# First pass of an attention with one shared key head: for long rows, the maximum of two key chunks taken through a rectified difference

## The chip, the cores and the metric

The kernel runs on one core of a Trainium2 chip. The metric is the device time of one launch in microseconds (us); lower is better. The core has TensorE (matrix products into PSUM), VectorE, ScalarE, GpSimd and DMA queues, each with its own program, kept in step by semaphores.

## The reference, cut to what matters

Two transformer layers with adaptive layer norms work on x of 2048 tokens by 256, fp32. The change is in the first attention:

```python
q = (h @ Wq).reshape(1, 2048, 16, 16)        # 16 heads of 16
k = h @ Wk; v = h @ Wv                       # one key and one value head for all
scores = einsum('bihd,bjd->bhij', q, k) / 4
attn = softmax(where(j <= i, scores, -inf))  # causal
out = einsum('bhij,bjd->bihd', attn, v) @ Wo + bo
```

The router, the expert layer, a second mixing layer and a second expert layer that follow are untouched.

## The kernel before

`phase_front` holds the whole first attention. Queries are cut into 4 chunks of 512 (index c) and heads into 4 groups of 4 (index g). The 16 groups s = (c, g) are worked in the order c = 0..3, within it g = 0..3. A group has 4(c+1) *units*, one for each tile of 128 keys (index kt), so there are 16, 32, 48 and 64 units for c = 0, 1, 2, 3, 160 in all, numbered u.

A unit does the second pass. For two pairs of heads TensorE makes scores with keys on the partitions (`scores`, L391, two halves of 8 matmuls; four matmuls of 32 output rows stand beside each other in the array and count as one quad). Each half fills one of two PSUM buffers `sc[0]`, `sc[1]`, ScalarE takes the exponential of it (L548, up to 128x1024), and TensorE multiplies the probabilities of the unit before with the values (`values`, L407). The half may be written when the exponential of the half two before has ended (`e_done`, L387). In the last four units of a group (the diagonal ones) only 512, 384, 256 and 128 query columns are left, and GpSimd masks a block (L791).

The exponent needs each query row's maximum beforehand. The first pass makes it: for each head of a group, tile of 128 queries and key chunk of 512 (index ck = 0..c) TensorE makes scores with queries on the partitions (`first_pass`, L348, one quad of up to 512 columns) into a ring of 3 PSUM banks. VectorE reduces them: with a plain `reduce_max` (L604) for ck < c, and for the diagonal chunk with a fused add of the causal mask and maximum (L601). These are 640 chunks: 384 plain, 256 diagonal. The partial maxima of a row meet in `mneg` (L608), are split in two bf16 parts and travel by DMA into two extra rows of the query operand, so that the second pass subtracts them in its product.

The order of all this is written out by `front_schedule`. The first pass runs ahead of the second: 44 chunks before unit 0, the rest spread evenly over the units so that a group's last chunk comes 5 units before the group starts, at most 5 chunks a unit. From unit 140 on there is none. Within a unit TensorE does: scores of half 0, one chunk, scores of half 1, two chunks, the values of the unit before, the remaining chunks, and now and then an output transposition or projection (kinds A, B, C; L357, L365, L374) that shares the ring.

Of the kernel before, what the change touches and what calls it, by code (L numbers as in the profile page):

```python
# [10 lines left out]
BF = mybir.dt.bfloat16  # L11
# [149 lines left out]
RING = 3  # L161
QLOADS = 3


def front_schedule():

    groups = [(c, g) for c in range(NC) for g in range(NG)]
    units = [(s, kt) for s, (c, g) in enumerate(groups) for kt in range(TQ * (c + 1))]
    chunks = [(s, hs, qt, ck) for s, (c, g) in enumerate(groups) for hs in range(GH)
              for qt in range(TQ * c, TQ * (c + 1)) for ck in range(c + 1)]  # L170
    start = [min(u for u, (t, kt) in enumerate(units) if t == s) for s in range(len(groups))]
    upto = [sum(t <= s for t, hs, qt, ck in chunks) for s in range(len(groups))]
    NU = len(units)

    due = [(-1, PRE)] + [(start[s] - 1 - MARGIN, upto[s]) for s in range(len(groups)) if upto[s] > PRE]
    due.append((NU - 1, len(chunks)))
    issued = [0] * NU
    for (u0, n0), (u1, n1) in zip(due, due[1:]):
        for u in range(u0 + 1, u1 + 1):
            issued[u] = n0 + (n1 - n0) * (u - u0) // (u1 - u0)  # L180
    for u in range(NU - 2, -1, -1):
        issued[u] = max(issued[u], issued[u + 1] - 5)
    ready = [PRE] + issued
    order = (("A", 0), ("A", 1), ("B", 0), ("A", 2), ("B", 1), ("C", 0), ("A", 3), ("B", 2), ("C", 1), ("B", 3),
             ("C", 2), ("C", 3))
    extras = {u: [] for u in range(NU + 1)}
    for c, (first, step) in enumerate(((start[4] + 2, 1), (start[8] + 2, 1), (start[15] - 4, 1))):
        for n, (kind, t) in enumerate(order):
            extras[first + step * n].append((kind, TQ * c + t))
    extras[NU] = [(kind, TQ * (NC - 1) + t) for kind, t in order]  # L190

    entries = []
    pre, n = [], 0
    for c in range(NC):
        for count in EARLY.get(c, ()):
            pre += [("P", n + j) for j in range(count)]
            n += count
        pre.append(("V", c))
    for m in range(PRE - n):
        pre.append(("P", n + m))  # L200
        if m % 2 == 0 and m // 2 < 6:
            pre.append(("M", m // 2))
    assert ("M", 5) in pre
    for e in pre:
        entries.append(e)
    per_unit = []
    for u in range(NU + 1):
        mine = [("P", n) for n in range(ready[u], ready[u + 1])] if u < NU else []
        first = len(entries)
        entries += mine + extras[u]  # L210
        per_unit.append((list(range(first, first + len(mine))), list(range(first + len(mine), len(entries)))))
    return groups, units, chunks, start, upto, entries, len(pre), per_unit


def phase_front(nc, k, a, sem, sb):
    groups, units, chunks, start, upto, entries, NPRE, per_unit = front_schedule()
    at = {e: r for r, e in enumerate(entries)}
    NU, NS = len(units), len(groups)
    diags = {u: n for n, u in enumerate(u for u, (s, kt) in enumerate(units) if kt >= TQ * groups[s][0])}
# [3 lines left out]
    with ctx:  # L223
# [14 lines left out]
        hT = k.h[:, 2 * TQ:4 * TQ, :].rearrange("p i d -> p (i d)").rearrange("p (s t n) -> p s t n", s=2, t=KH)  # L238
        parts = sb("q_parts", [P, 2, 3, KH, QC], BF)
        ks, vaug = sb("ks", [P, T], BF), sb("vaug", [P, NT, 32])  # L240
# [19 lines left out]
        pool_step = sem("f_pool_step")  # L260
        wqd_ready = sem("f_wqd_ready")
        silu_done, col_done, col_ready, wk_ready = sem("f_silu_done"), sem("f_col_done"), sem("f_col_ready"), sem("f_wk_ready")
        var1_ready, rstd1_ready, xh_ready = sem("f_var1_ready"), sem("f_rstd1_ready"), sem("f_xh_ready")
# [21 lines left out]
        def _(pe):  # L285
# [39 lines left out]
            def mod_rows(r, n):  # L325
# [7 lines left out]
                last.then_inc(ring_done, 1)  # L333

            def first_pass(r, n):
                s, hs, qt, ck = chunks[n]
                c, g = groups[s]
                diag = ck == c
                w = (qt % TQ + 1) * P if diag else QC
                free(r)  # L340
                if n == 0 or chunks[n - 1][0] != s:
                    pe.wait_ge(part_done, 9 * (c + 1))
                    pe.wait_ge(q_in[c], 16 * QLOADS)
                    if c == 0 and g:
                        pe.wait_ge(q_rest, 16 * QLOADS)
                for j in range(4):
                    q0 = P * (qt % TQ) + 32 * j
                    last = nc.tensor.matmul(bank(r)[32 * j:32 * (j + 1), 0:w], qs[0:KROWS, c, GH * g + hs, q0:q0 + 32],  # L348
                                            ks[0:KROWS, QC * ck:QC * ck + w], start=True, stop=True,
                                            tile_position=(0, 32 * j))  # L350
                last.then_inc(ring_done, 1)

# [29 lines left out]
            def scores(u, pair):  # L382
                s, kt = units[u]
                c, g = groups[s]
                off = max(0, kt - TQ * c) * P
                if u:
                    pe.wait_ge(e_done, 2 * u + pair - 1)  # L387
                for i in range(2):
                    for j in range(4):
                        k0 = P * kt + 32 * j  # L390
                        last = nc.tensor.matmul(sc[pair][32 * j:32 * (j + 1), i, off:QC], ks[0:KALL, k0:k0 + 32],  # L391
                                                qs[0:KALL, c, GH * g + 2 * pair + i, off:QC],
                                                start=True, stop=True, tile_position=(0, 32 * j))
                last.then_inc(s_done, 1)

            def values(u):
# [3 lines left out]
                if u in diags:  # L400
                    pe.wait_ge(masked, 2 * diags[u] + 2)
                else:
                    pe.wait_ge(e_done, 2 * u + 2)
                if kt == 0 and s:
# [46 lines left out]
            for u, (s, kt) in enumerate(units):  # L451
                mine, more = per_unit[u]
                if kt == 0:
                    pe.wait_ge(rows_in[s], 16 * NROWDMA)
                scores(u, 0)
                for r in mine[0:1]:
                    entry(r)
                scores(u, 1)
                for r in mine[1:3]:
                    entry(r)  # L460
# [9 lines left out]
        def _(act):  # L470
# [38 lines left out]
            def entry(r):  # L509
# [3 lines left out]
                if kind == "B":  # L513
                    copy_norm(r, n)

            def copy_out(s):
                c, g = groups[s]
# [23 lines left out]
            for u, (s, kt) in enumerate(units):  # L541
# [4 lines left out]
                for pair in range(2):  # L546
                    act.wait_ge(s_done, 2 * u + pair + 1)
                    nc.scalar.activation(prob[:, u % 2, 2 * pair:2 * pair + 2, off:QC], sc[pair][:, :, off:QC],  # L548
                                         ACT.Exp, scale=HD ** -0.5).then_inc(e_done, 1)
                if u - 1 in last_unit:  # L550
                    copy_out(last_unit[u - 1])
# [7 lines left out]
        def _(dve):  # L559
# [34 lines left out]
            def maxima(r, n):  # L594
                s, hs, qt, ck = chunks[n]
                c, g = groups[s]
# [3 lines left out]
                if ck == c:  # L600
                    nc.vector.tensor_tensor_reduce(unread[:, r % RING, 0:w], bank(r)[:, 0:w], causal[:, QC - w:QC], 1.0, NEG,  # L601
                                                   ALU.add, ALU.max, mpart[:, s % 2, hs, t, ck:ck + 1]).then_inc(ring_used[r % RING], 1)
                else:
                    nc.vector.reduce_max(mpart[:, s % 2, hs, t, ck:ck + 1], bank(r)[:, 0:w], AX.X).then_inc(ring_used[r % RING], 1)  # L604
                if n + 1 == upto[s]:
                    for m in range(max(0, r - RING + 1), r + 1):
                        dve.wait_ge(ring_used[m % RING], uses(m))
                    step(nc.vector.tensor_reduce(mneg[:, :, :], mpart[:, s % 2, :, :, 0:c + 1], axis=AX.X, op=ALU.max,  # L608
                                                 negate=True))
# [120 lines left out]
        def _(pool):  # L730
# [12 lines left out]
            for c in range(1, NC):  # L743
# [6 lines left out]
            nc.gpsimd.affine_select(out=causal[:, QC - P:QC], in_=causal[:, QC - P:QC], compare_op=ALU.is_ge, fill=NEG,  # L750
                                    base=0, pattern=[[-1, P]], channel_multiplier=1).then_inc(causal_set, 1)
            pool.wait_ge(pool_step, 3)
            nc.gpsimd.affine_select(out=k.before[:, :], in_=k.ones_bf[:, :], compare_op=ALU.is_gt, fill=0.0,
# [25 lines left out]
            for u, (s, kt) in enumerate(units):  # L779
# [6 lines left out]
                if u in diags:  # L786
                    off = (kt - TQ * groups[s][0]) * P
                    for pair in range(2):
                        pool.wait_ge(e_done, 2 * u + pair + 1)
                        block_ = prob[:, u % 2, 2 * pair:2 * pair + 2, off:off + P]  # L790
# [1363 lines left out]
```

## Time and profile before

| what | us |
|---|---|
| median of 3 runs | 1175.2 (1173.7 to 1178.07) |
| the profiled execution, own time | 1174.99 |
| its span, first to last instruction | 1173.2 |
| attention's exponentials (units 0 to 159), first start to last start | 94.3 to 516.3 |
| TensorE / VectorE / ScalarE busy, share of span | 84% / 54% / 46% |

The span is what an execution's trace covers; its own time is 1.8 us longer. Unit 28 starts (first exponential) at 175.1 us, unit 35 at 196.7, unit 92 at 354.6, unit 140 at 473.8. A busy share over the whole span mixes this stage with others; the stage must be read by itself.

### The profile page before, as it was taken

How to read it: one execution, taken by the hardware profiler on the slowest of the kernel's cores; microseconds unless marked ns; L12 is line 12 of the kernel's file. 1: busy time of each engine (PE TensorE's matmuls, PEld its weight loads, DVE VectorE, ACT ScalarE, POOL GpSimd, SP SyncE). 2: the span in 40 equal slices, each digit the busy share in tenths (PEclk: the TensorE clock that was granted, in tenths of full speed). 3: DMA queues.
4: the chain of work that ended last, by engine and by line, in shares of the span. 5: the costliest groups of instructions: out<-in, count | busy, mean ns of one | idle time of the engine just before them, and what ended most of it. 6: DMA issues, size and time to landing. Idle time of an engine off the chain costs nothing. (4 is left out here: it accounts for less than half of the span.)

```text
span 1173.2 us, 25043 instructions
## 1 busy us (share of the span) xinstructions
PE 980.0 (84%) x9915; PEld 633.0 (54%) x9919; DVE 631.1 (54%) x1710; ACT 534.2 (46%) x828; POOL 298.5 (25%) x344
## 2 busy tenths in 40 slices
PE   4897999999999999985079999649557599999994
PEld 2442343344334454432057777436435489999994
DVE  4257989999999999325100000185666533333331
ACT  2534665666667777754023222165045443333330
POOL 2004411100001100110512222245720045455442
PEclk9998999999999999997579999869788799999998
DMA  6765004000000000009315555300055722322233
GB/s 210 161 129 157 3 2 4 2 3 2 3 2 3 3 2 3 2 1 305 105 29 138 144 139 144 60 31 1 0 178 166 231 46 49 48 46 49 47 47 90
DMA packets 73406, 81.66 MB, mean 70 GB/s; under 512 B 23121, under 2 KB 64465, under 8 KB 72609
## 3 DMA queue, kind: packets, MB, share of 16 engines
q1 hardware_dynamic: 58912, 61.18, 18.7%
q0 software_dynamic: 12288, 17.10, 8.6%
q10 hardware_dynamic: 2112, 2.10, 0.6%
q8 instruction: 64, 1.05, 0.4%
q14 instruction: 30, 0.24, 0.1%
HBM read 58.19 MB, written 24.13 MB: 70 GB/s over the span
## 5 line engine op out<-in xcount | busy, mean ns | idle before, releaser
L548 ACT ACTIVATE k_prob<-f_s 128x1024 f32<-128x1024 f32 (+3 forms) x320 | 270.3, 896 | 136.1 <-PE f_s L391 135.6
L604 DVE TENSOR_REDUCE k_mpart<-f_r 128x1 f32<-128x512 f32 x384 | 250.2, 684 | 10.8 <-PE f_r L348 8.8
L348 PE MATMUL f_r<-k_ks,k_qs 112*32 112x512 bf16 (+3 forms) x2560 | 209.1, 353 | 17.0 <-DVE k_mpart L604 9.0
L391 PE MATMUL f_s<-k_qs,k_ks 114*32 114x512 bf16 (+3 forms) x2560 | 173.6, 349 | 5.1 <-ACT k_prob L548 3.7
L407 PE MATMUL f_o<-k_prob,k_vaug 128*32 128x512 f32 (+3 forms) x1280 | 147.9, 535 | 0.5 <-POOL k_prob L791 0.3
L348 PEld LDWEIGHTS f_r<-k_ks,k_qs 112*32 112x32 bf16 x2560 | 69.3, 95 | 146.3 <-DVE k_mpart L604 63.7
L601 DVE CUSTOM_DVE_ANT_0 k_unread<-f_r,k_causal 128x128 bf16<-128x128 f32 (+3 forms) x256 | 121.1, 483 | 28.2 <-PE f_r L348 26.6
L791 POOL TENSOR_SCALAR_AFFINE_SELECT k_prob<-k_prob 128x256 f32<-128x256 f32 x128 | 52.0, 411 | 320.1 <-ACT k_prob L548 318.7
L391 PEld LDWEIGHTS f_s<-k_qs,k_ks 114*32 114x32 bf16 x2560 | 64.9, 97 | 74.6 <-ACT k_prob L548 22.1
L1925 DVE TENSOR_TENSOR mid<-silu_g,e_u 128x512 f32<-128x512 f32 x39 | 26.8, 688 | 124.7 <-PE e_u L1830 124.7
L1365 DVE SCALAR_TENSOR_TENSOR outr<-p_o,rows,k_mod 128x256 f32<-128x256 f32 x16 | 7.7, 484 | 141.1 <-PE p_o L1322 141.1
L1830 PEld LDWEIGHTS e_g<-xT,wg 128*128 128x128 f32 x624 | 75.6, 192 | 3.3 <-ACT xT L1885 1.4
L1311 PE MATMUL p_h<-rowsT,k_wi 128*128 128x320 f32 x256 | 73.1, 445 | 4.9 <-issue 3.9
L1830 PE MATMUL e_g<-xT,wg 128*128 128x128 f32 x624 | 76.2, 275 | 0.9 <-ACT xT L1885 0.9
L1973 POOL DMA_INDIRECT xb<-h_rows,k_tok_of x39 | 45.1, 1156 | 124.0 <-PE e_x L1824 64.5
L1830 PE MATMUL e_u<-xT,wu 128*128 128x128 f32 x624 | 76.0, 275 | 0.0
L1982 POOL DMA_INDIRECT sum<-y,k_row_of x39 | 62.0, 1591 | 53.0 <-DVE y L1936 50.1
L1351 ACT ACTIVATE mid<-p_h 128x320 f32<-128x320 f32 x64 | 28.0, 437 | 103.0 <-PE p_h L1311 103.0
L1841 PE MATMUL e_y<-k_w1T,mid 128*128 x312 | 73.6, 379 | 0.0
L1830 PEld LDWEIGHTS e_u<-xT,wu 128*128 128x128 f32 x624 | 72.8, 192 | 0.0
L1311 PEld LDWEIGHTS p_h<-rowsT,k_wi 128*128 128x128 f32 x256 | 49.2, 195 | 26.6 <-issue 8.3
L1841 PEld LDWEIGHTS e_y<-k_w1T,mid 128*128 128x128 f32 x312 | 56.3, 190 | 6.1
(299 smaller groups left out, 1272.4 us busy)
## 6 DMA issues: line engine op xcount, KB each, us to landing
r_raw<-in_L_ffn_w_dram SPq DMA_DIRECT2D x24, 512.0 KB, 6.3
k_wi<-in_L_ffn_wi_dram SPq DMA_DIRECT2D x8, 1024.0 KB, 5.2
k_wo_e<-in_L_ffn_wo_dram SPq DMA_DIRECT2D x8, 1024.0 KB, 7.7
k_qs<-q_dram SPq DMA_DIRECT2D x6, 768.0 KB, 9.4
sum<-k_x SPq DMA_DIRECT2D x8, 512.0 KB, 7.3
q_dram<-k_q_parts SPq DMA_DIRECT2D x12, 256.0 KB, 6.6
disp<-k_wmod SPq DMA_DIRECT2D x2, 1310.0 KB, 6.4
rows<-disp SPq DMA_DIRECT2D x8, 262.0 KB, 2.7
```

What stands on the lines that cost most here:

```text
L348: last = nc.tensor.matmul(bank(r)[32 * j:32 * (j + 1), 0:w], qs[0:KROWS, c, GH * g + hs, q0:q0 + 32], ks[0:KROWS, QC * ck:QC * ck + w], st ...
L391: last = nc.tensor.matmul(sc[pair][32 * j:32 * (j + 1), i, off:QC], ks[0:KALL, k0:k0 + 32], qs[0:KALL, c, GH * g + 2 * pair + i, off:QC], ...
L407: last = nc.tensor.matmul(ot[32 * j:32 * (j + 1), off:QC], vaug[:, kt, :], prob[:, u % 2, j, off:QC], start=(kt == 0), stop=(kt == TQ * (c ...
L548: nc.scalar.activation(prob[:, u % 2, 2 * pair:2 * pair + 2, off:QC], sc[pair][:, :, off:QC], ACT.Exp, scale=HD ** -0.5).then_inc(e_done, 1)
L601: nc.vector.tensor_tensor_reduce(unread[:, r % RING, 0:w], bank(r)[:, 0:w], causal[:, QC - w:QC], 1.0, NEG, ALU.add, ALU.max, mpart[:, s % ...
L604: nc.vector.reduce_max(mpart[:, s % 2, hs, t, ck:ck + 1], bank(r)[:, 0:w], AX.X).then_inc(ring_used[r % RING], 1)
L791: nc.gpsimd.affine_select(out=block_, in_=block_, compare_op=ALU.is_ge, fill=0.0, base=0, pattern=[[0, 2], [1, P]], channel_multiplier=-1) ...
L1311: last = nc.tensor.matmul(ph[n % 2][:, :], wi[:, s, t, P * n:P * (n + 1)], rowsT[:, s, t, :], start=(t == 0), stop=(t == KH - 1))
L1830: last = nc.tensor.matmul(out[:, P * c:P * (c + 1)], w[:, s, F1 * t + P * c:F1 * t + P * (c + 1)], xT[:, s, t, :], start=(t == 0), stop=(t ...
L1841: last = nc.tensor.matmul(py[s][:, :], m[:, s, P * c:P * (c + 1)], k.w1T[:, e, 2, D * c:D * (c + 1)], start=(c == 0), stop=(c == FT - 1))
L1973: nc.gpsimd.indirect_dma_start(out=xb[:, s, :], out_offset=None, in_=k.h_rows, in_offset=bass.IndirectOffsetOnAxis(ap=k.tok_of[:, b:b + 1] ...
L1982: nc.gpsimd.indirect_dma_start(out=k.sum1, out_offset=bass.IndirectOffsetOnAxis(ap=k.row_of[:, b:b + 1], axis=0), in_=y[:, s, :], in_offse ...
```

## The change

For the query chunks c = 2 and c = 3 (`PAIRED = 2`) key chunk 0 has no first-pass chunk of its own any more. Since max(a, b) = max(a - b, 0) + b, the scores a with key chunk 0 and b with key chunk 1 are dealt with as follows. For a pair of rows (a row is one head and one tile of 128 queries) TensorE makes a - b for both (`pair_products`): for each row a quad with key chunk 0 and, added onto it in PSUM, a quad with the negated key chunk 1, both of 512 columns. This goes into one of the two buffers `sc` that the halves use, as a third turn behind the two halves of a unit. ScalarE keeps Relu of its 128x1024 in `over`, fp32, of which there are 3 copies (`keep_over`). In the unit after, or later, VectorE takes chunk 1 of each of the rows with the same fused add and maximum as the diagonal chunk, `over` in the mask's place. Such a turn is called K below. There are 64, two rows each. GpSimd negates key chunk 1 once, into the space of the query weights; `over` shares the space of the query parts, which are dead by then. The schedule's rule is as before; it now spreads 512 chunks, and places a K turn one unit ahead of the first use.

```diff
+        for n, (hs, qt) in enumerate(rows):
+            if c >= PAIRED and n % 2 == 0:
+                pairs.append([(s,) + row for row in rows[n:n + 2]])
+            for ck in range(c >= PAIRED, c + 1):
+                chunks.append((s, hs, qt, ck, (len(pairs) - 1, n % 2) if c >= PAIRED and ck == 1 else None))
...
+        copies = []
+        while k < len(pairs) and first_use[k] <= u + 1:
+            copies.append(k)
+            k += 1
+        if u < NU:
+            halves += [("E", u, 0), ("E", u, 1)] + [("K", m) for m in copies]
...
+            def turn_free(h):
+                if h >= 2:
+                    pe.wait_ge(e_done, h - 1)
+
+            def pair_products(k):
+                h = place[("K", k)]
+                turn_free(h)
+                pe.wait_ge(minus_keys, 1)
+                for i, (s, hs, qt) in enumerate(pairs[k]):
+                    queries(s)
+                    c, g = groups[s]
+                    for keys, first in ((ks[0:KROWS, 0:QC], True), (kneg[0:KROWS, :], False)):
+                        for j in range(4):
+                            q0 = P * (qt % TQ) + 32 * j
+                            last = nc.tensor.matmul(sc[h % 2][32 * j:32 * (j + 1), i, :], qs[0:KROWS, c, GH * g + hs, q0:q0 + 32],
+                                                    keys, start=first, stop=not first, tile_position=(0, 32 * j))
+                last.then_inc(s_done, 1)
...
                 scores(u, 1)
+                for k_ in copies:
+                    pair_products(k_)
                 for r in mine[1:3]:
                     entry(r)
...
+            def keep_over(k):
+                h = place[("K", k)]
+                act.wait_ge(s_done, h + 1)
...
+                if k >= COPIES:
+                    for r in mates[k - COPIES]:
+                        act.wait_ge(ring_used[r % RING], uses(r))
+                nc.scalar.activation(over[:, k % COPIES, :, :], sc[h % 2][:, :, :], ACT.Relu).then_inc(e_done, 1)
...
+                elif mate:
+                    k_, i = mate
+                    dve.wait_ge(e_done, place[("K", k_)] + 1)
+                    nc.vector.tensor_tensor_reduce(unread[:, r % RING, :], bank(r)[:, :], over[:, k_ % COPIES, i, :], 1.0, NEG,
+                                                   ALU.add, ALU.max, mpart[:, s % 2, hs, t, ck:ck + 1]).then_inc(ring_used[r % RING], 1)
...
+            pool.wait_ge(part_done, 9 * 2)
+            pool.wait_ge(wqd_ready, KH)
+            nc.gpsimd.tensor_scalar(kneg[:, :], ks[:, QC:2 * QC], -1.0, None, ALU.mult).then_inc(minus_keys, 1)
```

The halves' waits and buffers are renumbered: a half's place h in the common order of halves and K turns takes the place of 2u + pair.

## Rows read from the trace of the kernel before

**Rows 1.** The page, part 2: busy tenths in 40 slices of the span.

```profile
PE   4897999999999999985079999649557599999994
DVE  4257989999999999325100000185666533333331
```

**Rows 2.** Windows: length, then busy us (and instructions) of each engine, clock, DMA.

```profile
core 0: us, PE busy (x) PEld busy (x) DVE busy (x) ACT busy (x) POOL busy (x), PEclk, DMA share, GB/s
94.00:140.40 46.40, 36.89 (x644) 16.08 (x648) 42.63 (x131) 22.71 (x36) 26.40 (x43) 0.93 0.27 83
...
196.60:473.80 277.20, 269.82 (x4348) 120.18 (x4352) 265.19 (x624) 188.29 (x222) 26.71 (x65) 1.00 0.01 2
...
354.60:473.80 119.20, 117.43 (x1928) 56.98 (x1924) 114.07 (x253) 86.67 (x99) 9.61 (x24) 1.00 0.01 2
...
473.80:518.30 44.50, 41.81 (x520) 15.46 (x512) 7.70 (x27) 35.53 (x46) 7.43 (x17) 1.00 0.01 2
```

**Rows 3.** Groups by form, 354.6 to 473.8: busy us, mean ns, idle before.

```profile
L604 DVE TENSOR_REDUCE k_mpart<-f_r 128x1 f32<-128x512 f32 x144 | 92.2, 685 | 4.3 <-PE f_r L348 3.5
L548 ACT ACTIVATE k_prob<-f_s 128x1024 f32<-128x1024 f32 x78 | 75.7, 1024 | 25.4 <-PE f_s L391 25.4
L601 DVE CUSTOM_DVE_ANT_0 k_unread<-f_r,k_causal 128x512 bf16<-128x512 f32 x13 | 8.9, 688 | 0.1
```

**Rows 4.** Timeline of TensorE, unit 137: start, us, matmuls in a row.

```profile
465.38 0.27 PE L348 MATMUL f_r<-k_ks,k_qs 112*32 112x128 bf16 x4
465.44 0.64 PE L391 MATMUL f_s<-k_qs,k_ks 114*32 114x512 bf16 x8
465.87 0.43 PE L348 MATMUL f_r<-k_ks,k_qs 112*32 112x512 bf16 x4
466.09 0.65 PE L391 MATMUL f_s<-k_qs,k_ks 114*32 114x512 bf16 x8
466.52 0.65 PE L348 MATMUL f_r<-k_ks,k_qs 112*32 112x512 bf16 x8
466.96 1.08 PE L407 MATMUL f_o<-k_prob,k_vaug 128*32 128x512 f32 x8
467.82 0.33 PE L348 MATMUL f_r<-k_ks,k_qs 112*32 112x256 bf16 x4
467.93 0.65 PE L391 MATMUL f_s<-k_qs,k_ks 114*32 114x512 bf16 x8
```

**Rows 5.** Timeline of ScalarE: a group's first unit, then units 137 to 139.

```profile
404.30 1.94 ACT L548 ACTIVATE k_prob<-f_s 128x1024 f32<-128x1024 f32 x2 [1.92 <-PE f_s L391]
...
466.19 1.94 ACT L548 ACTIVATE k_prob<-f_s 128x1024 f32<-128x1024 f32 x2 [0.50 <-PE f_s L391]
468.69 1.94 ACT L548 ACTIVATE k_prob<-f_s 128x1024 f32<-128x1024 f32 x2 [0.56 <-PE f_s L391]
471.23 1.94 ACT L548 ACTIVATE k_prob<-f_s 128x1024 f32<-128x1024 f32 x2 [0.61 <-PE f_s L391]
```

**Rows 6.** Timeline of ScalarE and TensorE behind it, units without first pass.

```profile
502.94 1.02 ACT L548 ACTIVATE k_prob<-f_s 128x1024 f32<-128x1024 f32 x1 [0.96 <-PE f_s L391]
...
504.01 0.12 PEld L391 LDWEIGHTS f_s<-k_qs,k_ks 114*32 114x32 bf16 x8 [0.80 <-ACT k_prob L548]
504.93 0.12 PEld L391 LDWEIGHTS f_s<-k_qs,k_ks 114*32 114x32 bf16 x8 [0.80 <-ACT k_prob L548]
```

**Rows 7.** Waits, 196.6 to 354.6: us in total, times, longest.

```profile
PEld f_r L348 <- DVE k_mpart L604: 38.6, 98, 1.6
...
PEld f_r L348 <- DVE k_mpart L601: 7.9, 26, 0.5
```

**Rows 8.** Waits, 354.6 to 473.8, the same two lines.

```profile
PEld f_r L348 <- DVE k_mpart L604: 10.5, 27, 1.4
...
PEld f_r L348 <- DVE k_mpart L601: 2.6, 8, 0.4
```

**Rows 9.** Line L548 by itself: durations ns min/median/max, and its table load.

```profile
L548 ACT ACTIVATE k_prob<-f_s x320: 378/1018/1072, 94.3 to 516.3; 128x1024 f32<-128x1024 f32 x112, 128x768 f32<-128x768 f32 x16, 128x512 f32<-128x512 f32 x16, 128x256 f32<-128x256 f32 x16
L548 ACT ACT_TABLE_LOAD  x1: 1283/1283/1283, 93.0 to 93.0; - x1
```

**Rows 10.** Windows (columns of rows 2) early in the stage.

```profile
105.00:110.00 5.00, 1.70 (x38) 0.55 (x30) 4.68 (x14) 2.23 (x3) 3.49 (x5) 1.00 0.41 165
110.00:115.00 5.00, 4.63 (x60) 1.76 (x56) 4.70 (x15) 2.20 (x4) 3.16 (x4) 0.66 0.91 375
```

**Rows 11.** Window 60 to 75: GpSimd before the stage.

```profile
60.00:75.00 15.00, 13.86 (x122) 6.25 (x122) 10.17 (x48) 5.84 (x9) 0.00 (x0) 1.00 0.35 81
```

More of the change, by code:

```diff
@@ L162 @@
 QLOADS = 3
+COPIES = 3
+PAIRED = 2
+ORDER = [(c, g) for c in range(NC) for g in range(NG)]
 def front_schedule():
-    groups = [(c, g) for c in range(NC) for g in range(NG)]
+    groups = list(ORDER)
     units = [(s, kt) for s, (c, g) in enumerate(groups) for kt in range(TQ * (c + 1))]
-    chunks = [(s, hs, qt, ck) for s, (c, g) in enumerate(groups) for hs in range(GH)
-              for qt in range(TQ * c, TQ * (c + 1)) for ck in range(c + 1)]
+    chunks, pairs = [], []
+    for s, (c, g) in enumerate(groups):
+        rows = [(hs, qt) for hs in range(GH) for qt in range(TQ * c, TQ * (c + 1))]
+        for n, (hs, qt) in enumerate(rows):
[3 more added lines that the diff above has]
+                chunks.append((s, hs, qt, ck, (len(pairs) - 1, n % 2) if c >= PAIRED and ck == 1 else None))
     start = [min(u for u, (t, kt) in enumerate(units) if t == s) for s in range(len(groups))]
-    upto = [sum(t <= s for t, hs, qt, ck in chunks) for s in range(len(groups))]
+    upto = [sum(ch[0] <= s for ch in chunks) for s in range(len(groups))]
     NU = len(units)
@@ L186, in front_schedule @@
     extras = {u: [] for u in range(NU + 1)}
[L187 to L190, printed above, removed]
+    for s, (c, g) in enumerate(groups):
+        if (c, g) == [t for t in groups if t[0] == c][-1]:
+            first = (start[4] + 2, start[8] + 2, start[15] - 4, NU)[c]
+            for n, (kind, t) in enumerate(order):
+                extras[min(first + n, NU)].append((kind, TQ * c + t))
     entries = []
@@ L205, in front_schedule @@
         entries.append(e)
-    per_unit = []
+    first_use = {}
+    for n, ch in enumerate(chunks):
+        if ch[4]:
+            first_use.setdefault(ch[4][0], min(u for u in range(NU) if issued[u] > n))
+    per_unit, halves, k = [], [], 0
     for u in range(NU + 1):
@@ L210, in front_schedule @@
         entries += mine + extras[u]
-        per_unit.append((list(range(first, first + len(mine))), list(range(first + len(mine), len(entries)))))
-    return groups, units, chunks, start, upto, entries, len(pre), per_unit
+        copies = []
[4 more added lines that the diff above has]
+            halves += [("E", u, 0), ("E", u, 1)] + [("K", m) for m in copies]
+        per_unit.append((list(range(first, first + len(mine))), list(range(first + len(mine), len(entries))), copies))
+    assert k == len(pairs)
+    return groups, units, chunks, pairs, halves, start, upto, entries, len(pre), per_unit
 def phase_front(nc, k, a, sem, sb):
-    groups, units, chunks, start, upto, entries, NPRE, per_unit = front_schedule()
+    groups, units, chunks, pairs, halves, start, upto, entries, NPRE, per_unit = front_schedule()
     at = {e: r for r, e in enumerate(entries)}
+    place = {e: h for h, e in enumerate(halves)}
+    mates = {k: [at[("P", n)] for n, ch in enumerate(chunks) if ch[4] and ch[4][0] == k] for k in range(len(pairs))}
+    last_of = {c: max(s for s, (cc, g) in enumerate(groups) if cc == c) for c in range(NC)}
     NU, NS = len(units), len(groups)
@@ L238, in phase_front @@
         hT = k.h[:, 2 * TQ:4 * TQ, :].rearrange("p i d -> p (i d)").rearrange("p (s t n) -> p s t n", s=2, t=KH)
-        parts = sb("q_parts", [P, 2, 3, KH, QC], BF)
+        kneg = wq[:, 0, :].bitcast(BF)
+        over = sb("over", [P, COPIES, 2, QC])
+        parts = over[:, :, :, :].rearrange("p s i n -> p (s i n)").bitcast(BF)\
+            .rearrange("p (c s t n) -> p c s t n", c=2, s=3, t=KH)
         ks, vaug = sb("ks", [P, T], BF), sb("vaug", [P, NT, 32])
@@ L261, in phase_front @@
         wqd_ready = sem("f_wqd_ready")
+        minus_keys = sem("f_minus_keys")
         silu_done, col_done, col_ready, wk_ready = sem("f_silu_done"), sem("f_col_done"), sem("f_col_ready"), sem("f_wk_ready")
@@ L333, in mod_rows, with queries, maxima_product @@
                 last.then_inc(ring_done, 1)
+            def queries(s):
+                c, g = groups[s]
+                pe.wait_ge(part_done, 9 * (c + 1))
+                pe.wait_ge(q_in[c], 16 * QLOADS)
+                if c == 0 and g:
+                    pe.wait_ge(q_rest, 16 * QLOADS)
+            def maxima_product(dst, s, hs, qt, ck, w):
+                c, g = groups[s]
+                for j in range(4):
+                    q0 = P * (qt % TQ) + 32 * j
+                    last = nc.tensor.matmul(dst[32 * j:32 * (j + 1), :], qs[0:KROWS, c, GH * g + hs, q0:q0 + 32],
+                                            ks[0:KROWS, QC * ck:QC * ck + w], start=True, stop=True,
+                                            tile_position=(0, 32 * j))
+                return last
+            def turn_free(h):
[7 more added lines that the diff above has]
+                    queries(s)
+                    c, g = groups[s]
+                    for keys, first in ((ks[0:KROWS, 0:QC], True), (kneg[0:KROWS, :], False)):
+                        for j in range(4):
+                            q0 = P * (qt % TQ) + 32 * j
+                            last = nc.tensor.matmul(sc[h % 2][32 * j:32 * (j + 1), i, :], qs[0:KROWS, c, GH * g + hs, q0:q0 + 32],
+                                                    keys, start=first, stop=not first, tile_position=(0, 32 * j))
+                last.then_inc(s_done, 1)
             def first_pass(r, n):
-                s, hs, qt, ck = chunks[n]
+                s, hs, qt, ck, mate = chunks[n]
                 c, g = groups[s]
@@ L341, in first_pass @@
                 if n == 0 or chunks[n - 1][0] != s:
[L342 to L351, printed above, removed]
+                    queries(s)
+                maxima_product(bank(r)[:, 0:w], s, hs, qt, ck, w).then_inc(ring_done, 1)
             def out_turn(r, i):
@@ L385, in scores @@
                 off = max(0, kt - TQ * c) * P
-                if u:
-                    pe.wait_ge(e_done, 2 * u + pair - 1)
+                h = place[("E", u, pair)]
+                turn_free(h)
                 for i in range(2):
@@ L390, in scores @@
                         k0 = P * kt + 32 * j
-                        last = nc.tensor.matmul(sc[pair][32 * j:32 * (j + 1), i, off:QC], ks[0:KALL, k0:k0 + 32],
+                        last = nc.tensor.matmul(sc[h % 2][32 * j:32 * (j + 1), i, off:QC], ks[0:KALL, k0:k0 + 32],
                                                 qs[0:KALL, c, GH * g + 2 * pair + i, off:QC],
@@ L402, in values @@
                 else:
-                    pe.wait_ge(e_done, 2 * u + 2)
+                    pe.wait_ge(e_done, place[("E", u, 1)] + 1)
                 if kt == 0 and s:
@@ L451, in _ @@
             for u, (s, kt) in enumerate(units):
-                mine, more = per_unit[u]
+                mine, more, copies = per_unit[u]
                 if kt == 0:
@@ L514, in entry @@
                     copy_norm(r, n)
+            def keep_over(k):
+                h = place[("K", k)]
+                act.wait_ge(s_done, h + 1)
+                if k == 0:
+                    for part in range(3):
+                        act.wait_ge(spilled[part], 16 * NC)
+                if k >= COPIES:
+                    for r in mates[k - COPIES]:
+                        act.wait_ge(ring_used[r % RING], uses(r))
+                nc.scalar.activation(over[:, k % COPIES, :, :], sc[h % 2][:, :, :], ACT.Relu).then_inc(e_done, 1)
             def copy_out(s):
@@ L546, in _ @@
                 for pair in range(2):
-                    act.wait_ge(s_done, 2 * u + pair + 1)
-                    nc.scalar.activation(prob[:, u % 2, 2 * pair:2 * pair + 2, off:QC], sc[pair][:, :, off:QC],
+                    h = place[("E", u, pair)]
+                    act.wait_ge(s_done, h + 1)
+                    nc.scalar.activation(prob[:, u % 2, 2 * pair:2 * pair + 2, off:QC], sc[h % 2][:, :, off:QC],
                                          ACT.Exp, scale=HD ** -0.5).then_inc(e_done, 1)
+                for k_ in per_unit[u][2]:
+                    keep_over(k_)
                 if u - 1 in last_unit:
@@ L594, in maxima @@
             def maxima(r, n):
-                s, hs, qt, ck = chunks[n]
+                s, hs, qt, ck, mate = chunks[n]
                 c, g = groups[s]
@@ L607, in maxima @@
                         dve.wait_ge(ring_used[m % RING], uses(m))
-                    step(nc.vector.tensor_reduce(mneg[:, :, :], mpart[:, s % 2, :, :, 0:c + 1], axis=AX.X, op=ALU.max,
+                    step(nc.vector.tensor_reduce(mneg[:, :, :], mpart[:, s % 2, :, :, (c >= PAIRED):c + 1], axis=AX.X, op=ALU.max,
                                                  negate=True))
@@ L788, in _ @@
                     for pair in range(2):
-                        pool.wait_ge(e_done, 2 * u + pair + 1)
+                        pool.wait_ge(e_done, place[("E", u, pair)] + 1)
                         block_ = prob[:, u % 2, 2 * pair:2 * pair + 2, off:off + P]
```

## The prediction

> **What bounds the kernel now.** I begin with the page's slices. Over the fifth to the sixteenth of them both TensorE and VectorE stand at 9 tenths [rows 1], so a share cannot say which is the bound. The windows narrow it: where the changed query chunks' first pass lies, 196.6 to 473.8 us (units 35 to 139), TensorE is busy 269.8 of 277.2 us, VectorE 265.2, ScalarE 188.3, at a granted clock of 1.00 [rows 2]. So I look at single units. In unit 137 TensorE's instructions start one behind the other: 0.43 to 0.44 us after a start with 8 matmuls the next begins, and 0.22 after one with 4 (465.87 to 466.09); the durations shown (0.43, 0.65) hold a tail that the next one covers [rows 4]. A quad of 512 columns thus takes a slot of 0.2165 us of TensorE (466.09 to 466.52 is two). The values take 0.86 (466.96 to 467.82), four slots. Unit 137 is 4 + 4 slots of scores and values and 1792 first-pass columns, 3.5 slots: 11.5 x 0.2165 = 2.49 us, and from 465.44 to 467.93 it took 2.49; the exponentials start 2.50 and 2.54 us apart [rows 5]. There is no gap. TensorE is the bound in these units, by its slots. VectorE's four chunks there need three times 0.65 us (a 685 ns row overlaps its neighbour by 0.04) and one shorter, 2.2 to 2.6 us, so it is close behind [rows 3]. That is why both look full.
>
> Summed over units 35 to 139 from the code's column counts: 380,928 columns of scores and values plus 203,648 of first pass (445 chunks) are 584,576 columns, 1142 slots, 247 us of the 277. The other 30 are output turns and projections (12 entries, some 9 us by my estimate), the ends of groups, where ScalarE idles 1.92 us before a new group's first exponential instead of 0.5 to 0.6 [rows 5] (eight of them at about 1.5, so 12), and some 9 in which TensorE really waits for VectorE. The waits listed for VectorE are larger, 38.6 + 7.9 before 354.6 and 10.5 + 2.6 after [rows 7, 8], but they are waits of weight loads, and lie mostly under running matmuls.
>
> **The change part by part.**
>
> *TensorE's products.* Removed: 128 chunks of key chunk 0 (8 groups x 16 rows), 128 slots. Added: 64 K turns with 2 rows x 2 key sets = 4 slots each, 256. Net 128 slots x 0.2165 = **+27.7 us**, on the path in a stage whose bound is TensorE. An accumulating quad is not in these rows; I take the slot of a plain one, since the columns streamed are the same. Bounds: 0 extra for it, or each second quad as long as it shows when nothing follows, 0.43 instead of 0.22, 128 x 0.21 = 27 more [rows 4]. I take 0.
>
> *The wait that K adds.* K is written as the third turn of two buffers, right behind half 1. Its buffer is the one whose exponential belongs to half 0 of the same unit. The exponential starts 0.75 us after the scores' first matmul (465.44 to 466.19) [rows 4, 5], takes 1.02, and TensorE resumes 0.05 after its end (502.94 + 1.02 = 503.96, weight load at 504.01) [rows 6]: 1.82 us after half 0 began. TensorE has half 0, one chunk and half 1 to fill this, 5 slots or 1.08 us. It is then blocked for 0.74 us, in program order: two chunks, the values and the next unit's scores stand behind K. By my count of the schedule 47 K turns fall into units of full width; 17 into diagonal ones, where the scores, the tail and the exponential (0.378 at the narrowest [rows 9]) are all shorter: 0.42 at the narrowest, some 0.52 on average. 47 x 0.74 + 17 x 0.52 = **+43.6 us**. Bounds: 0, if something already there covers it, and 64 x 1.4 = 90, if a second wait for the Relu follows. I keep 43.6, as the sums come from rows of the same units.
>
> *ScalarE.* 64 Relu of 128x1024 at an exponential's 1.02 us [rows 3] are +65 us, 188 becomes 253 of some 330. In a unit with K: exponentials end at 1.77 and 2.69, K's products are ready at 1.82 + 0.75 + 0.43 = 3.0, the Relu ends at 4.0. The next half 0 starts at about 3.95 and its exponential at 4.7. So ScalarE doesn't delay the chain: 0, hidden under TensorE's slots. If Relu cost 30% more, it would end at 4.3 and still be hidden.
>
> A Relu among exponentials might need its table reloaded: 128 loads at 1.283 us = 164. The trace has one load on this line, though copies of other kinds stand between its 320 exponentials [rows 9]; none is a Relu. That makes it a rival, with a small chance since none of the other kinds needed a load. The Trainium skill ("ScalarE: Activation LUTs", section "Table sets: the hidden batching unit") says that cheap functions, relu among them, are in every table set; by it the term is 0; no row of this trace shows a Relu.
>
> *VectorE.* 128 reductions go, 128 x 0.65 = 83 us less. 128 others become the fused form, 688 against 685 ns at 512 columns [rows 3]: 0. The new wait for `over` is met a unit ahead. VectorE drops to about 182 us, off the bound. What comes back is only what TensorE truly waited for it: bounds 0 and 21 (the 30 without the output turns), I take **-10 us**. TensorE's slots are late next.
>
> *The rest.* K turns in diagonal units partly fall into waits that the group ends have anyway: **-5 us** (bounds 0 and -9, all 17 turns). GpSimd's negation of 128x512 comes when key chunk 1 is ready; GpSimd has nothing from 60 to 75 us [rows 11]; 0, and if it came later, it would have 20 of 46.4 us free [rows 2]. If it were late it would hold K at unit 35, 100 us on. No DMA is added or moved past another. The last 20 units have no first pass and are unchanged; so are the later layers.
>
> *The clock.* It fell to a mean of 0.66 in 110 to 115 after TensorE had been busy only 1.70 of 5 us [rows 10]. Waits of under 1 us between the exponentials at 502.94 to 504.93 [rows 6] left it at 1.00 [rows 2]. K's waits are of that size: 0. If it averaged 0.93, as over 94 to 140.4 [rows 2], the 290 us of slots would take 20 more.
>
> Sum: 27.7 + 43.6 - 10 - 5 = +56 us, on the profiled execution's 1175.0 (span 1173.2 + 1.8), which is the median of the runs to 0.2: **1231 us**.
>
> **The rivals.**
>
> *A. K's wait is covered.* ScalarE would have to run ahead, or half 0's exponential end within 1.08 us of its scores. For it: the wait is short, and queues can shift. Against: 0.75 + 1.02 is fixed by rows. Time: 1175 + 28 - 10 = 1193 us; it decides if K's quads start within 0.1 us of half 1's.
>
> *B. Two waits for each K.* If the Relu's end (4.0 us into the unit) held half 1 of the next, or its exponentials queued behind it, some 0.6 us more per turn: 1231 + 38 = 1269 us. For: in two successive K units ScalarE has three turns each. Against: the Relu ends 0.6 before half 1 of the next wants its buffer (3.95 + 0.65).
>
> *C. Faster.* The weight loads' waits for VectorE, 46.5 + 13.1 = 59.6 us [rows 7, 8], are real idle time of the array. Then 27.7 us of new slots fit in, and the time falls by up to 59.6 - 27.7 = 32, to 1143 us, if K's wait is covered too. It decides in units 76 to 91, where five chunks a unit need over 2.8 us of VectorE. For: exponentials before 354.6 lie further apart than TensorE's slots. Against: TensorE is busy 269.8 of 277.2 us [rows 2], and K's wait alone eats the rest.
>
> *D. Table loads.* 1231 + 164 = 1395 us.
>
> *E. The change doesn't bite*, K so rare or so placed that gains and losses cancel: about 1175. Against: 64 turns, all within 105 units.
>
> **How the numbers follow.** Forecast 75 in 100; A 9; B 9; C 4; D 1; E 2. A measurement of this kernel can tell about 0.5% (6 us) from no change. Faster: C, 0.04. Within: E and 1 of A, 0.03. The rest slower, 0.93. The forecast's own range, from the bounds of the VectorE term, half of K's wait and the accumulating quads, is 1210 to 1252; reaching towards A, 1202 to 1252 holds 8 in 10.
>
> **What would show it.** In the profile after: ScalarE has 64 Relu of about 1.02 us and no new table load; VectorE's busy time in the stage falls by some 80 us; TensorE's rows show, in each unit with K, a gap of about 0.7 us between half 1 and K's 16 matmuls, put down to the exponential; units with K are about 3.9 us apart and those without about 2.3; unit 140 starts some 56 us later than 473.8, and what follows keeps its length. I am wrong if K's quads follow half 1 without a gap, if a quad added to another takes no slot of its own, or if the units with K take under 3.2 us.

## The result, and the profile after

The changed kernel takes 1228.1 us (median of 4 runs, 1227.3 to 1229.4) against 1176.6 for the kernel before (median of 4, of which the first three are those with the median 1175.2): slower by 51.5 us. The ratio is 1.045 (95% interval 1.043 to 1.047), which is 1228.1 against 1175.2. The forecast was 1231, 56 us more than 1175. The profiled execution has a span of 1226.0 us, 52.8 more than before. One run of the last experiment below took 1670 us at a mean granted clock of 0.586, where all others have 0.93 to 0.94, and is left out of its ratio.

The whole difference lies between units 28 and 140: by the exponentials' starts (the last unit to its first exponential), units 0 to 27 take 81.4 us (80.9 before), units 28 to 139 351.8 (298.7), units 140 to 159 42.2 (42.1). Unit 140 starts at 526.4. The windows of the kernel after, units 35 to 139 and the units without first pass (columns as in [rows 2]):

```profile
193.10:526.40 333.30, 299.61 (x4884) 125.54 (x4880) 198.52 (x636) 253.15 (x287) 26.63 (x65) 1.00 0.01 2
...
526.40:571.10 44.70, 41.80 (x520) 15.30 (x513) 7.28 (x25) 35.49 (x46) 7.42 (x17) 1.00 0.01 2
```

Against [rows 2] VectorE does 67 us less (265.2 to 198.5), ScalarE 65 more (188.3 to 253.2), and TensorE 30 more. TensorE's busy share falls from 0.97 to 0.90 although it has more to do. So work was added to it, and waits. The granted clock stayed at 1.00. From the page after, section 5 (L394 is K's products, L583 the Relu, L678 the fused add and maximum, L681 the plain reduction; `k_over` is `over`):

```profile
L394 PE MATMUL f_s<-k_ks,k_qs 112*32 112x512 bf16 x512 | 50.8, 384 | 33.0 <-ACT k_prob L618 33.0
L583 ACT ACTIVATE k_over<-f_s 128x1024 f32<-128x1024 f32 x64 | 65.6, 1025 | 23.7 <-PE f_s L394 23.7
L678 DVE CUSTOM_DVE_ANT_0 k_unread<-f_r,k_over 128x512 bf16<-128x512 f32 x128 | 88.2, 689 | 58.9 <-PE f_r L374 58.4
L681 DVE TENSOR_REDUCE k_mpart<-f_r 128x1 f32<-128x512 f32 x128 | 88.0, 687 | 40.8 <-PE f_r L374 40.7
```

The fused form costs what the plain reduction costs (689 and 687 ns), and both now wait for TensorE (58.4 and 40.7 us). A Relu takes 1025 ns like an exponential; the exponentials' line still has one table load, at 91.8 us. The mechanism is in TensorE's timeline (start, length, matmuls, idle before), unit 133 and the beginning of 134; `k_wq` is the space in which the negated keys now lie:

```profile
504.74 0.60 PE L446 MATMUL f_s<-k_qs,k_ks 114*32 114x512 bf16 x8
505.17 0.39 PE L374 MATMUL f_r<-k_ks,k_qs 112*32 112x512 bf16 x4
505.39 0.60 PE L446 MATMUL f_s<-k_qs,k_ks 114*32 114x512 bf16 x8
506.53 0.40 PE L394 MATMUL f_s<-k_ks,k_qs 112*32 112x512 bf16 x4 [0.54 <-ACT k_prob L618]
506.76 0.39 PE L394 MATMUL f_s<-k_wq,k_qs 112*32 112x512 bf16 x4
506.97 0.39 PE L394 MATMUL f_s<-k_ks,k_qs 112*32 112x512 bf16 x4
507.19 0.39 PE L394 MATMUL f_s<-k_wq,k_qs 112*32 112x512 bf16 x4
507.40 0.50 PE L374 MATMUL f_r<-k_ks,k_qs 112*32 112x512 bf16 x8
507.73 1.03 PE L462 MATMUL f_o<-k_prob,k_vaug 128*32 128x512 f32 x8
508.59 0.60 PE L446 MATMUL f_s<-k_qs,k_ks 114*32 114x512 bf16 x8
```

Half 1 begins at 505.39 and has its two slots until 505.82; K begins at 506.53. The 0.71 us between are the wait for half 0's exponential; the row says 0.54, since the tail of the matmul before counts as busy. K's four quads start 0.21 to 0.23 us apart, one slot each, added onto another or not. The unit takes 3.85 us (504.74 to 508.59), the next, without K, 2.33; before, two successive units took 5.04 [rows 5]. Measured so for all 64 turns (K's start less the end of the slots before it), the wait is 43.4 us in all: 0.70 in the middle, 0.38 to 0.97.

### The profile page after: what moved, and what is told of

Read it like the earlier page. It is cut to its first block and busy times, and to the rows that moved or that the text cites. A ratio compares the mean times of both kernels' runs of the same rounds, so it can differ in the third digit from the quotient of the medians.

```text
span 1226.0 us, 26516 instructions
## 1 busy us (share of the span) xinstructions
PE 1009.8 (82%) x10427; PEld 639.8 (52%) x10431; DVE 560.7 (46%) x1710; ACT 599.1 (49%) x892; POOL 299.4 (24%) x345
## 5 line engine op out<-in xcount | busy, mean ns | idle before, releaser
L374 PE MATMUL f_r<-k_ks,k_qs 112*32 112x512 bf16 (+3 forms) x2048 | 157.5, 343 | 11.5 <-DVE k_mpart L673 5.7
L871 POOL TENSOR_SCALAR_AFFINE_SELECT k_prob<-k_prob 128x256 f32<-128x256 f32 x128 | 51.5, 408 | 373.5 <-ACT k_prob L618 372.2
L446 PEld LDWEIGHTS f_s<-k_qs,k_ks 114*32 114x32 bf16 x2560 | 61.9, 97 | 104.3 <-issue 42.5
L678 DVE CUSTOM_DVE_ANT_0 k_unread<-f_r,k_over 128x512 bf16<-128x512 f32 x128 | 88.2, 689 | 58.9 <-PE f_r L374 58.4
L681 DVE TENSOR_REDUCE k_mpart<-f_r 128x1 f32<-128x512 f32 x128 | 88.0, 687 | 40.8 <-PE f_r L374 40.7
L374 PEld LDWEIGHTS f_r<-k_ks,k_qs 112*32 112x32 bf16 x2048 | 53.1, 96 | 85.3 <-issue 17.3
L394 PE MATMUL f_s<-k_ks,k_qs 112*32 112x512 bf16 x512 | 50.8, 384 | 33.0 <-ACT k_prob L618 33.0
L583 ACT ACTIVATE k_over<-f_s 128x1024 f32<-128x1024 f32 x64 | 65.6, 1025 | 23.7 <-PE f_s L394 23.7
```

Of the source, the lines that this page charges most:

```text
L374: last = nc.tensor.matmul(dst[32 * j:32 * (j + 1), :], qs[0:KROWS, c, GH * g + hs, q0:q0 + 32], ks[0:KROWS, QC * ck:QC * ck + w], start=Tr ...
L446: last = nc.tensor.matmul(sc[h % 2][32 * j:32 * (j + 1), i, off:QC], ks[0:KALL, k0:k0 + 32], qs[0:KALL, c, GH * g + 2 * pair + i, off:QC], ...
L583: nc.scalar.activation(over[:, k % COPIES, :, :], sc[h % 2][:, :, :], ACT.Relu).then_inc(e_done, 1)
L678: nc.vector.tensor_tensor_reduce(unread[:, r % RING, :], bank(r)[:, :], over[:, k_ % COPIES, i, :], 1.0, NEG, ALU.add, ALU.max, mpart[:, s ...
```

## The experiments

Each was timed beside the kernel before, whose median was 1173.3 us for the first four below, 1175.2 for the next four and 1176.6 for the last. Ratios are to that median. A difference to the changed kernel's 1228.1 crosses sessions that lie up to 3 us apart, so the stage is given beside it: units 28 to 139 of the profiled execution, 298.7 us before, 351.8 changed.

**The wait in front of K, moved.**

```diff
                 scores(u, 1)
+                if u:
+                    values(u - 1)
                 for k_ in copies:
                     pair_products(k_)
                 for r in mine[1:3]:
                     entry(r)
-                if u:
-                    values(u - 1)
```

> The changed kernel with one move on TensorE: in a unit with a K turn, the values of the unit before are multiplied ahead of K and not behind it. The same matmuls, the same work on ScalarE and VectorE. Theory (the cost is 128 net slots plus a blocked wait of 0.7 us in front of each K): K then starts 1.94 us after half 0, behind the exponential's end at 1.82, so the wait in front of K goes; the Relu ends at about 4.1 and holds half 1 of the next unit for some 0.3. Net 0.4 us a turn, 64 turns, -26 us: 1202. Rival (ScalarE's 65 us of Relu set the pace): the Relu now starts later relative to the next unit, so no gain or a loss, 1225 to 1235.

Measured: 1208.9 us, ratio to before 1.030 (1.028 to 1.031), 19 us under the changed kernel where 26 were expected. The stage is 328.4 us, 23.4 less than changed. The edit moves the values in every unit and not only, as the expectation has it, in those with K: units 0 to 27, which have no K, take 84.5 us, against 80.5 to 82.3 in all others. That is 3 of the missing 7 us; the stage itself misses 2.6. K's wait is gone (sum over 64 turns: none). TensorE in this kernel, and then its weight loads' waits from 196 to 525 us (line waited for: us in total, times, longest):

```profile
496.16 0.61 PE L446 MATMUL f_s<-k_qs,k_ks 114*32 114x512 bf16 x8
496.59 1.03 PE L462 MATMUL f_o<-k_prob,k_vaug 128*32 128x512 f32 x8
497.45 0.39 PE L394 MATMUL f_s<-k_ks,k_qs 112*32 112x512 bf16 x4
...
499.18 0.39 PE L374 MATMUL f_r<-k_ks,k_qs 112*32 112x512 bf16 x4
499.62 0.61 PE L446 MATMUL f_s<-k_qs,k_ks 114*32 114x512 bf16 x8
```

```profile
PEld f_s L446 <- ACT k_over L583: 31.3, 55, 1.0
PEld f_s L394 <- ACT k_prob L618: 30.4, 59, 0.7
```

K now follows the values at once (496.59 + 0.86 = 497.45). A new wait stands in front of the next unit's half 1, which wants the buffer the Relu still reads: 499.40 to 499.62 here. Both rows are of weight loads, and lie in part under running matmuls, the 30.4 under the values. Changed, the first was 3.0 us. By the starts, TensorE stands still for some 17 us of the stage between a chunk and the scores behind it, 2 in the changed kernel. With two buffers and three turns a wait moves on rather than vanishes. The rival, no gain, is out.

**K's slots, halved.**

```diff
-                    for keys, first in ((ks[0:KROWS, 0:QC], True), (kneg[0:KROWS, :], False)):
+                    for keys, first in ((ks[0:KROWS, 0:QC], True),):
...
-                                                    keys, start=first, stop=not first, tile_position=(0, 32 * j))
+                                                    keys, start=True, stop=True, tile_position=(0, 32 * j))
```

> The changed kernel without the quads of the negated key chunk (this part of the computation is left out): a K turn has 2 slots on TensorE instead of 4; waits, Relu and VectorE's work stay. Theory: K's wait stays at 0.7 us and 128 slots of 0.2165 go, -27.7 us: 1200. Rival (ScalarE sets the pace, TensorE's slots lie in its shadow): within 5 us of 1228.

Measured: 1200.4 us, 1.023 (1.021 to 1.025): 27.8 under the changed kernel, and 27.7 in the stage (324.2); 128 slots are 27.7. K's waits still sum to 43.3. So slots and wait are two prices that add up, and in the changed kernel each slot is paid in full.

**No K turn at all.** The K turns' list is left empty, and key chunk 1 is reduced with `reduce_max`. The maximum over key chunk 0 is thus left out.

> The changed kernel with no K turn at all and a plain reduction of key chunk 1: key chunk 0 is left out of the maxima of the long rows. Against the kernel before, only removals: 128 slots of TensorE, 83 us of VectorE. Theory: -27.7 for the slots and -10 for the waits for VectorE: 1138. Rival (VectorE bounds the stage before): up to -60, 1116. Rival (no wait for VectorE was real): -27.7, 1149.

Measured: 1140.3 us, 0.973 (0.970 to 0.976), 33 under the kernel before; expected 38. The stage is 263.2 us, 35.5 less than before: 27.7 for the slots, 7.8 for waits. TensorE's matmuls waited 7 us for VectorE before and 0.7 now, but they have a new wait at the start of groups, for the DMA that brings the maxima:

```profile
PE f_s L446 <- DMA k_qs<-k_m2t: 6.4, 6, 1.6
```

From here to the changed kernel are 88.6 us of stage: 256 slots (55.4) and 33.2 net for the waits. Of K's 43.4 us some 10 thus fell into time in which TensorE waits anyway in the kernel without turns. The wait for the DMA, of which the changed kernel has none, can be 6.4 of it.

**The slots alone, in the kernel before.**

```diff
+                if c >= 2 and ck == 0:
+                    for j in range(4):
+                        q0 = P * (qt % TQ) + 32 * j
+                        last = nc.tensor.matmul(bank(r)[32 * j:32 * (j + 1), 0:w], ...
...
                 last.then_inc(ring_done, 1)
```

> The kernel before, in which the quad of key chunk 0 of the long rows is computed twice into the same bank: 128 slots more on TensorE, nothing else. It measures the slots by themselves. Theory: +27.7, less what fits into TensorE's waits for VectorE (0 to 12): 1192 to 1204. Rival (weight loads' waits of 60 us for VectorE are idle time of the array): within 5 us of 1176.

Measured: 1193.0 us, 1.017 (1.015 to 1.019): +19.7, the stage +17.4. Of 27.7 us of slots 8 to 10 fit into waits. Between the rivals this decides: most of the waits listed in [rows 7, 8], 59.6 us, are not idle time of the array. The trace of before has the right rows, those of the matmuls (PE) in place of the weight loads (PEld); with all lines for VectorE they come to 7.1 us from unit 28 to 139:

```profile
PE f_r L348 <- DVE k_mpart L604: 6.1, 19, 0.8
...
PE f_r L348 <- DVE k_mpart L601: 0.4, 2, 0.2
```

**VectorE's work alone, in the kernel before.**

```diff
-                    nc.vector.reduce_max(..., bank(r)[:, 0:w], AX.X)...
+                    nc.vector.reduce_max(..., bank(r)[:, 0:(32 if c >= 2 and ck == 0 else w)], AX.X)...
```

> The kernel before, in which the reduction of key chunk 0 of the long rows takes 32 columns of 512 (the rest of its maxima is left out): about 128 x 0.5 = 64 us less on VectorE, TensorE unchanged. It measures what the removal of VectorE's work is worth by itself. Theory: 8 to 12 us, 1163 to 1166. Rival (VectorE bounds the stage): 30 us and more, under 1145.

Measured: 1166.8 us, 0.993 (0.991 to 0.996): 8.4 less (the interval allows 5 to 11), the stage 8.7 less, 3.1 of it in units 76 to 91 with five chunks each, 3.6 in units 33 to 46, 1.3 in units 92 to 139. VectorE's busy time fell by 55 us (631.1 to 576.5), and this is the whole worth of it. VectorE's idle before its full reductions is then 38.8 us from 196 to 470 us, nearly all for TensorE:

```profile
L604 DVE TENSOR_REDUCE k_mpart<-f_r 128x1 f32<-128x512 f32 x192 | 127.1, 688 | 38.8 <-PE f_r L348 37.6
```

**Half the dose.** `PAIRED = 3`.

> The changed kernel with PAIRED = 3: only query chunk 3 has K turns, 32 of the 64. Theory (a fixed price per turn of 2 net slots and a wait): units 80 to 139 lose about 27 us as in the changed kernel, units 33 to 79 none: 1200. Rival (the loss comes from something once, like the shared space or the early schedule): near 1176 or near 1226.

Measured: 1200.2 us, 1.023 (1.019 to 1.027), as expected. Units 33 to 75 take what they took before to 0.4 us, units 76 to 91 6.0 us more, units 92 to 139 20.8 more, the very number of the changed kernel. Half the turns cost half, 26.4 us of the stage against 53.1: the price is one per turn.

**Half the Relu.** The Relu takes 256 of each row's 512 columns.

> The changed kernel whose Relu takes only the first 256 of each row's 512 columns (half of the kept values is left out), 0.6 us instead of 1.02, 27 us less on ScalarE; TensorE and VectorE as changed. Theory (ScalarE is hidden): the changed kernel's time, 1224 to 1228. Rival (ScalarE sets the pace of units with K): up to 27 us less, 1201.

Measured: 1226.9 us, 1.044 (1.040 to 1.047). The stage is 351.2 us, against 351.8, with a Relu of 598 ns. ScalarE's own time is hidden in the changed kernel.

**The difference through the ring.** A row's difference is an entry of the first pass's ring, behind the values (its two quads as in `pair_products`, but into `bank(r)`); ScalarE frees the bank:

```diff
+        turns = [("R", (m, i)) for m in copies for i in range(2)]
...
+        entries += mine + turns + extras[u]
...
+                nc.scalar.activation(over[:, k % COPIES, i, :], bank(r)[:, :], ACT.Relu).then_inc(ring_used[r % RING], 1)
```

> The changed kernel in which each row's difference goes not into the halves' buffers but into a bank of the first pass's ring, at the end of a unit, and ScalarE takes 128 Relu of 128x512 from there instead of 64 of 128x1024. The same slots on TensorE, the same VectorE work, somewhat more on ScalarE; no wait for an exponential in front of the difference. Theory (slots and blocked wait are two separate costs): the kernel without K turns, 1140, plus 256 slots of 0.2165 = 55: 1196, up to 1202 with waits at the ring. Rival (ScalarE's Relu work or the hand-over to VectorE costs the 33 us): 1220 to 1235.

Measured: 1186.5 us, 1.011 (1.007 to 1.015), 42 under the changed kernel with all its slots and more work on ScalarE, and 10 under what was expected. The place of the wait is shown: it was the buffer's, neither the Relu's nor the hand-over's. The expectation was 10 us too high because it paid all 256 slots: the stage is 310.8 us, 47.6 over the kernel without turns and not 55.4. That kernel's 6.4 us of waits for the maxima's DMA are gone here, so slots went into them. Against before the stage is 12.1 over; of 27.7 us of net slots 15.6 are hidden. TensorE in a unit with two differences, without a gap:

```profile
399.92 1.05 PE L478 MATMUL f_o<-k_prob,k_vaug 128*32 128x512 f32 x8
400.78 0.41 PE L410 MATMUL f_r<-k_ks,k_qs 112*32 112x512 bf16 x4
401.00 0.40 PE L410 MATMUL f_r<-k_wq,k_qs 112*32 112x512 bf16 x4
401.21 0.41 PE L410 MATMUL f_r<-k_ks,k_qs 112*32 112x512 bf16 x4
401.43 0.41 PE L410 MATMUL f_r<-k_wq,k_qs 112*32 112x512 bf16 x4
401.64 0.62 PE L462 MATMUL f_s<-k_qs,k_ks 114*32 114x512 bf16 x8
```

**The key difference made once.** On top of the ring: the keys of chunk 1 are taken from those of chunk 0 once, so that a row's difference is one quad.

```diff
+            def key_difference(r, n):
+                for sign in range(2):
+                    last = nc.tensor.matmul(bank(r)[:, :], sel[0:KROWS, sign, :], ks[0:KROWS, QC * sign:QC * (sign + 1)],
+                                            start=(sign == 0), stop=(sign == 1))
+                last.then_inc(diff_done, 1)
+                for part in range(1, 3):
+                    pe.wait_ge(diff_kept, part)
+                    last = nc.tensor.matmul(bank(r)[:, :], minus[:, part, :], kneg[:, :], start=False, stop=True,
+                                            skip_group_check=True)
...
+                for keys, first in ((kneg[0:KROWS, :], True),):
```

> The kernel whose rows' differences go through the ring, with one more change: the difference of key chunks 0 and 1 is made once (in unit 5: two products with a 0/1 matrix that adds up the three bf16 parts of a key, then cut into parts again on ScalarE with two products that take the parts away), and a row's difference is one quad with it instead of two. TensorE has as many slots as before the change, VectorE 83 us less, no wait for an exponential in front of the difference. Theory (slots at 0.2165 us are paid in full, the rest is hidden): 1186 - 27.7 + 3 for the preparation = 1162, about 13 us faster than the kernel before. Rival (with ScalarE at 75 us more the stage is bound by ScalarE and nothing comes back below the time before): 1173 to 1180.

Measured: 1172.0 us, 0.9959 (0.9946 to 0.9973): 0.4% under the kernel before, so it beats both, but 10 us above what was expected. The stage is 292.7 us, 6.0 less than before and 18.1 less than through the ring. A window (columns as in [rows 2]), ScalarE, and then TensorE over the same two units:

```profile
355.00:470.00 115.00, 113.67 (x1852) 46.26 (x1852) 83.45 (x244) 106.66 (x142) 8.51 (x22) 1.00 0.01 3
```

```profile
452.26 1.08 ACT L606 ACTIVATE k_over<-f_r 128x512 f32<-128x512 f32 x2 [0.18 <-PE f_r L398]
453.23 4.00 ACT L653 ACTIVATE k_prob<-f_s 128x1024 f32<-128x1024 f32 x4
457.41 1.09 ACT L606 ACTIVATE k_over<-f_r 128x512 f32<-128x512 f32 x2 [0.18 <-PE f_r L398]
```

```profile
451.82 0.61 PE L398 MATMUL f_r<-k_wq,k_qs 112*32 112x512 bf16 x8
452.25 0.61 PE L465 MATMUL f_s<-k_qs,k_ks 114*32 114x512 bf16 x8
452.68 0.39 PE L379 MATMUL f_r<-k_ks,k_qs 112*32 112x512 bf16 x4
452.90 0.61 PE L465 MATMUL f_s<-k_qs,k_ks 114*32 114x512 bf16 x8
453.34 0.55 PE L379 MATMUL f_r<-k_ks,k_qs 112*32 112x512 bf16 x8
453.72 1.03 PE L481 MATMUL f_o<-k_prob,k_vaug 128*32 128x512 f32 x8
454.58 0.61 PE L465 MATMUL f_s<-k_qs,k_ks 114*32 114x512 bf16 x8
455.01 0.39 PE L379 MATMUL f_r<-k_ks,k_qs 112*32 112x512 bf16 x4
455.23 0.61 PE L465 MATMUL f_s<-k_qs,k_ks 114*32 114x512 bf16 x8
455.67 0.61 PE L379 MATMUL f_r<-k_ks,k_qs 112*32 112x512 bf16 x8
456.11 1.03 PE L481 MATMUL f_o<-k_prob,k_vaug 128*32 128x512 f32 x8
456.97 0.61 PE L398 MATMUL f_r<-k_wq,k_qs 112*32 112x512 bf16 x8
```

ScalarE runs four exponentials and two Relu in 5.15 us with 0.18 idle, and its idle time ends with TensorE's difference. TensorE's starts follow without a gap: from 451.82 to 456.97 it has 23.75 slots (the one at 453.34 is a quad of 512 and one of 384 columns), 5.14 us of 5.15. So TensorE is still the bound here, with ScalarE close behind, and the rival, which has ScalarE as the bound, is not borne out. What failed in the expectation is its sum. It took 128 slots in full off the time through the ring, where 15.6 us of slots were hidden already. In the stage this kernel has as many slots as the kernel before; the kernel without turns plus 128 slots is 263.2 + 27.7 = 290.9 us, and 292.7 was measured. At most some 2 us are left for everything else, ScalarE included. The gain over before, 6.0 us of the stage, is mostly the waits for VectorE: TensorE's matmuls wait 2.4 us for it, 7.1 before.

## Why the prediction was right

*The bound.* Read as TensorE by its slots, unit by unit. Shown from both sides: slots added alone cost 19.7 of 27.7 us, and taking 55 us of VectorE's busy time away alone is worth 8.4.

*Slots, +27.7.* Taking one quad of each row's two out gave 27.7 in the stage. The low bound of the accumulating quad held: it takes one slot.

*K's wait, +43.6.* Measured 43.4 over the 64 turns, 0.71 where 0.74 was worked out. The chain of 0.75, 1.02 and 0.05 us against five slots was the step on which the forecast stood. It came from rows of two different stretches, unit 137 and the units without first pass, and not all of the same units as the prediction says.

*ScalarE, 0.* Halving the Relu moved nothing (1226.9), so hidden as said. Even with the slots paid back and 128 smaller Relu, TensorE's slots still set the time of two units, 5.14 of 5.15 us.

*VectorE's return, -10.* 7.8 net in the kernel without turns, 8.4 to 8.7 with short reductions. In the range; the forecast took a little too much. VectorE's busy time fell by 67 and not some 80 us: with gaps between them, its instructions no longer overlap at their ends.

*Turns in waits at the groups' ends, -5.* Mis-sized by half: with 53.1 us for the stage, 27.7 + 43.4 - 7.8 leaves -10.2 here. The time that swallows K's wait is also of another kind than the forecast has it: up to 6.4 us of it are waits for the maxima's DMA, which appear once VectorE's work and the slots are gone. Which turns met which wait was not traced. The 5 us too few here and the 2 too many for VectorE partly cancel, so the sum of 56 came out 3 us over the stage's 53.1. That closeness is in part luck; the two large terms, 27.7 and 43.6, are not.

*The rivals.* A: K's wait was not covered; where the order or the place covers it, the time is 1208.9 and 1186.5 (A said 1193). B: waits of half 1 for the Relu were 3.0 us in all. C: the idle time that was to take in the new slots is 8 to 10 us, not 59.6. D: no table load more. E: the change cost 51.5 us. The units with K take 3.85 us in the rows above (forecast 3.9), those without 2.33 (2.3).

## What to carry to other kernels

When two engines both look full, work out one period from the slots of each: the one whose starts follow without a gap is the bound, and an exchange that relieves the other costs what it adds here. A further turn on a pair of buffers has a price of its own, the round trip of the turn two before less the work in between; put it where that work is long enough, or into buffers whose user is free, before counting gains. And start each sum from slots and real waits, not from another version's time: what that version hid is not paid back when it is taken out, and this made one expectation here 10 us too hopeful. For the real waits of TensorE, read the rows of its matmuls (7 us) and not those of its weight loads (59.6); they are somewhat low, since the tail of the matmul before counts as busy (33.0 us in the row for K's waits, 43.4 by the starts).

## What the runs showed of the hardware

A quad that adds onto another in PSUM starts 0.21 to 0.23 us after it, as one that overwrites. A Relu of 128x1024 from PSUM took 1025 ns and one of 128x512 598; with 64 of the former among 320 exponentials there was no table load but the one in front of the first exponential, as before. TensorE's waits of 0.4 to 1.0 us, 64 of them, left the granted clock at 1.00 throughout the stage.
